# First batch of the second attention: its second half of scores in two projection banks, both weighings read ahead of the sums, POOL's four differences in a row

## Chip, cores, metric

The kernel runs on 1 core of one Trainium2 chip. The metric is the device time of one execution, in microseconds (us), as the median of several runs.

## What is computed

Thirty-two batches of 128 tokens with 128 features pass through two layers, each a cross attention and a mixture of experts. The change lies in the second layer's attention (16 heads of 64):

```python
x = x + _L0_xattn_ref(_layernorm(x), ctx_768, mask_BxS_bk0, L0_xattn_Wq, L0_xattn_Wkv)
x = x + _L0_ffn_ref(_layernorm(x), ...)          # 8 experts, top 2
x = x + _L1_xattn_ref(_layernorm(x), ctx_768, w_q, w_k, w_v, w_out, b_out)
x = x + _L1_ffn_ref(_layernorm(x), ...)          # 16 experts, top 1, and a shared one

def _L1_xattn_ref(x, cond, w_q, w_k, w_v, w_out, b_out):
    q = (x @ w_q).reshape(B, SQ, 16, 64)
    k = (cond @ w_k).reshape(B, SKV, 16, 64)
    v = (cond @ w_v).reshape(B, SKV, 16, 64)
    attn = softmax(einsum('bqhd,bkhd->bhqk', q, k) / 8)
    return einsum('bhqk,bkhd->bqhd', attn, v).reshape(B, SQ, 1024) @ w_out + b_out
```

## The kernel before, in words

The whole program is written out by hand, one instruction list for each engine, held together by semaphores. Five stages follow one another: the first attention, the first experts, the second attention (batches 0 to 31, steps of `attention()` on each engine), and the second experts with the shared one. Batch b of the second attention has two halves of eight heads (h = 0, 1), and each half two groups of four heads (g = 0 to 3). For a half:

- `coarse_half(b, h)` (TensorE, line 1311): scores in bf16 into the banks mf[0:2]. `half_max` (VectorE, L2164) takes their maxima over the keys; there is one pair of such banks, so a coarse half waits until the half before it has been reduced.
- `turn(b)` (TensorE, L1347 and L1353): transposes the maxima of batch b+1 and the normalized rows of a later batch into mf; ScalarE copies them out (L1762, L1772, L1773, L1776). At b = 0 the rows are those of batches 2 and 3, at b = 1 those of batch 4, so `turn(1)` waits for `normal_before(4)`.
- `score_half(b, h)` (L1284, then L1294 with the negated maxima): scores in fp32 into the banks S1 = sf[0:2]; ScalarE's `exponential` (L1755) writes them to pT[h] and counts `exp_done`. With one S1, a score half waits for the exponential of the half before it.
- `high_half` (VectorE L2158 or, for h = 0 of batches 1 to 6, ScalarE L1815): pT[h] rounded to bf16 in ph[h].
- `low_halves(b, h)` (POOL, L870, two instructions): pl[h] = pT[h] - ph[h].
- `weigh(b, g)` (TensorE, L1330, 16 matmuls): the weights, high and low, times the values, into the single bank of; `evacuate(b, g)` (VectorE, L2148 and L2149) divides by the row sums and frees the bank. So `weigh` of a group waits for `evacuate` of the group before it (`pv_free`) and for one of POOL's differences (`pl_done`).

Queries (`q0`, `q1`, L1223), transposed outputs (`oT0`, `oT1`, L1218) and the output product (`y`, L1214) go through three projection banks, J1 = sf[2], sf[3], jf; sf[2] and sf[3] are the two that the title names.

Beside this run the sums of the first experts: POOL's `fetch(t)` (L859, two gathers) brings two expert rows for batch t, VectorE's `combine(t)` (L2194, two instructions, all operands in SBUF) adds them to x, `stats_before` and `aggregate_before` (L2205, L2209, L2210) take mean and variance, POOL's `root_before(t)` (L878) the inverse root, VectorE's `normal_before(t)` (L2217) the normalized rows, and POOL's `bias(t)` (L890) adds the output bias to x once `normal_before(t)` has read it. `normal_after` (L2233) does the same for the rows after the attention.

Orders written out by hand around the change:

- TensorE: ... coarse(0,1), q1 of batch 1, products of scores (0,0), turn(-1), shift of (0,0), coarse(1,0), scores (0,1), coarse(1,1), turn(0), weigh(0,0), q0 of batch 2, weigh(0,1); then step b = 1: scores (1,0), coarse(2,0), weigh(0,2), q1 of batch 2, oT0 of batch 0, weigh(0,3), scores (1,1), coarse(2,1), weigh(1,0), oT1 of batch 0, q0 of batch 3, weigh(1,1), y of batch 0, turn(1); then step 2 with scores (2,0), coarse(3,0), weigh(1,2), q1 of batch 3, oT0 of batch 1, weigh(1,3), and so on.
- POOL in step 1: root_before(4), low_halves(1,0), bias(4), fetch(7), low_halves(1,1); in step 2: root_before(5), root_after(0), low_halves(2,0), bias(5), fetch(8), low_halves(2,1).
- VectorE in step 1: evacuate(0,2), half_max(2,0), evacuate(0,3), statistics of batch 5, evacuate(1,0), half_max(2,1), high_half(1,1), evacuate(1,1), combine(6), the output and statistics of batch 0, normal_before(5).

Of the kernel before, what the change touches and what calls it, by code (L numbers as in the profile page):

```python
# [10 lines left out]
ACT = mybir.ActivationFunctionType  # L11
# [3 lines left out]
P = 128  # L15
# [129 lines left out]
def inside(b):  # L145
    return 0 <= b < NB
# [132 lines left out]
def build(nc, a, out):  # L279
    ctx = ExitStack()  # L280
    with ctx:
# [157 lines left out]
        bank = [sf[:, n, :] for n in range(4)] + [mf[:, n, :] for n in range(2)] + [of[:, :]]  # L439
        cf0, cf = sf[:, 0, 0:P // 2].bitcast(BF16), mf[:, 0, 0:P // 2].bitcast(BF16)  # L440
        S1, M1p, J1 = sf[:, 0:2, :], mf, [sf[:, 2, :], sf[:, 3, :], jf[:, :]]
        s_bank, st_bank, pj_bank = bank[0:2], bank[2:4], bank[4:6]
        o_bank = [of[:, 0:QH * (D1 + 1)], mf[:, 0, 0:QH * (D1 + 1)]]
        g_bank, y_bank = bank[0:4], (of[:, 0:DM], jf[:, 0:DM])
# [86 lines left out]
        with nc.Block(no_gpsimd_drain=True) as block:  # L531
# [200 lines left out]
            def _(pool):  # L732
# [140 lines left out]
                def attention():  # L873

                    def root_before(t):

                        pool.wait_ge(L1.veA_done, t + 1)
                        nc.gpsimd.tensor_tensor(rsA[:, t:t + 1], veA[:, t:t + 1], mhalf[:, 0:1], ALU.pow)\  # L878
                            .then_inc(L1.rsA_done, 1)

                    def root_after(n):

                        pool.wait_ge(L1.veF_done, n + 1)
                        nc.gpsimd.tensor_tensor(rstd[:, n:n + 1], veF[:, n:n + 1], mhalf[:, 0:1], ALU.pow)\
                            .then_inc(L1.rsF_done, 1)

                    def bias(t):

                        pool.wait_ge(L1.xn_ready, t + 1)
                        nc.gpsimd.tensor_tensor(x[:, t, :], x[:, t, :], bo1[:, :], ALU.add).then_inc(L1.biased, 1)  # L890

                    def score(q):

                        c = slice(QH * q, QH * q + QH)
                        pool.wait_ge(sel_ready, NROUNDS + q + 1)
                        nc.gpsimd.tensor_tensor(v2[:, c], einv[:, :], v1[:, c], ALU.pow).then_inc(scored, 1)

                    pool.wait_ge(tiles_ready, 3)
                    pool.wait_ge(cleared, 16 * NCLEAR)
                    store_tiles(0, SOON_TILES[0] + X0)  # L900
                    fetch(0)
                    store_tiles(SOON_TILES[0] + X0, SOON_TILES[0] + X0 + 4)
                    fetch(1)
                    store_tiles(SOON_TILES[0] + X0 + 4, SOON_TILES[0] + X0 + 8)
                    root_before(0)
                    store_tiles(SOON_TILES[0] + X0 + 8, SOON_TILES[2] + 4)
                    root_before(1)
                    store_tiles(SOON_TILES[2] + 4, SOON_TILES[2] + X0)
                    fetch(2)
                    store_tiles(SOON_TILES[2] + X0, SOON_TILES[2] + X0 + 4)  # L910
                    fetch(3)
                    store_tiles(SOON_TILES[2] + X0 + 4, SOON_TILES[2] + X0 + 12)
                    bias(0)
                    bias(1)
                    store_tiles(SOON_TILES[2] + X0 + 12, NT0 - X0)
                    root_before(2)
                    root_before(3)
                    store_tiles(NT0 - X0, NT0)
                    fetch(4)
                    fetch(5)  # L920
                    low_halves(0, 0)
                    fetch(6)
                    bias(2)
                    low_halves(0, 1)
                    bias(3)
                    for b in range(1, NB):
                        if inside(b + 3):
                            root_before(b + 3)
                        if inside(b - 2):
                            root_after(b - 2)  # L930
                        if b % QH == 0 and 0 <= b // QH - 2:
                            score(b // QH - 2)
                        if inside(b):
                            low_halves(b, 0)
                        if inside(b + 3):
                            bias(b + 3)
                        if inside(b + 6):
                            fetch(b + 6)
                        if inside(b):
                            low_halves(b, 1)  # L940
                    score(NQD - 2)
                    root_after(LAST - 1)
                    root_after(LAST)
                    score(NQD - 1)
# [23 lines left out]
            def _(pe):  # L968
# [231 lines left out]
                def fill(name, n):  # L1200

                    what, h, p = name[:-1], int(name[-1] == "1"), n % 2
                    bk, use = FILL1[name, n]
                    ps = J1[bk]
                    need(pe, L1.pj_free[bk], use)
                    if name == "q0" and n >= 3:
                        pe.wait_ge(L1.k_free, 2 * (n - 1) + 2)
                    if name == "oT0" and inside(n + 2):
                        pe.wait_ge(L1.k_free, 2 * (n + 2) + 2)
                    if name == "y":  # L1210
                        L1.free(pe, "oT0", n)
                        L1.free(pe, "oT1", n)
                        for c in range(NCH):
                            last = nc.tensor.matmul(ps[:, 0:DM], oT[:, c, :], wo1[:, c, :], start=(c == 0), stop=(c == NCH - 1))  # L1214
                    elif what == "oT":
                        pe.wait_ge(L1.pv_free, 4 * n + 2 * h + 2)
                        for c in range(4):
                            last = nc.tensor.transpose(ps[:, c * P:(c + 1) * P],  # L1218
                                                       o1[p][:, 8 * h + 2 * c:8 * h + 2 * c + 2, :], ident[:, :])
                    else:  # L1220
                        pe.wait_ge(L1.moved_done, MOVED1[XMOVE[n]] + 1)
                        for c in range(4):
                            last = nc.tensor.matmul(ps[:, c * P:(c + 1) * P], wq1[:, (4 * h + c) * P:(4 * h + c + 1) * P],  # L1223
                                                    xrn[p][:, :], start=True, stop=True)
                    last.then_inc(L1.pj_full[bk], 1)
# [47 lines left out]
                def score_products(b, h):  # L1273

                    p = b % 2
                    L1.free(pe, f"q{h}", b)
                    keys_there(b, h, L1.kf_io[p])
                    if h == 0 and b >= NKV:
                        pe.wait_ge(L1.v_free, 2 * b + 2)
                    need(pe, L1.exp_done, 2 * b + h)  # L1280
                    for n in range(4):
                        for r in range(2):
                            rr = slice(D1 * r, D1 * r + D1)
                            nc.tensor.matmul(S1[:, r, n * P:(n + 1) * P], kT[p][rr, 4 * h + n, :], qT[p][rr, 4 * h + n, :],  # L1284
                                             start=(n == 0), stop=False)

                def score_shift(b, h):
# [3 lines left out]
                    for n in range(4):  # L1291
                        for r in range(2):
                            rr = slice(D1 * r, D1 * r + D1)
                            last = nc.tensor.matmul(S1[:, r, n * P:(n + 1) * P], sel1[rr, 4 * h + n, :], cT1[p][rr, :],  # L1294
                                                    start=False, stop=(n == 3))
                            if n == 3:
                                last.then_inc(L1.s_full, 1)
# [305 lines left out]
            def _(act):  # L1603
# [146 lines left out]
                def exponential(b, h):  # L1750

                    act.wait_ge(L1.s_full, 4 * b + 2 * h + 2)
                    if b >= 1:
                        act.wait_ge(L1.pl_done, 4 * (b - 1) + 2 * h + 2)
                    nc.scalar.activation(pT[h][:, :, :, :].rearrange("p r c n -> p r (c n)"), S1, ACT.Exp, scale=D1 ** -0.5)\  # L1755
                        .then_inc(L1.exp_done, 1)

                def turn(b):
# [152 lines left out]
            def _(dve):  # L1911
# [353 lines left out]
                def attention():  # L2265
# [6 lines left out]
                    high_half(0, 0)  # L2272
                    half_max(1, 1)
                    high_half(0, 1)
                    combine(4)
                    stats_before(4)
                    aggregate_before(4)
                    evacuate(0, 0)
                    combine(5)
                    evacuate(0, 1)  # L2280
                    normal_before(4)

                    for b in range(1, LIGHT):
                        evacuate(b - 1, 2)
                        half_max(b + 1, 0)
                        evacuate(b - 1, 3)
                        stats_before(b + 4)
                        aggregate_before(b + 4)
# [1 line left out]
                        half_max(b + 1, 1)  # L2290
                        high_half(b, 1)
                        evacuate(b, 1)
                        if inside(b - 2):
                            normal_after(b - 2)
                        combine(b + 5)
# [339 lines left out]
```

## Time and profile before

| | |
|---|---|
| median of 3 runs | 936.29 us (935.24, 936.29, 941.63) |
| profiled execution | 932.35 us, span of its trace 930.7 us |
| TensorE | busy 844.5 us, 91% of the span, granted clock 0.964 on average |
| VectorE, ScalarE, POOL | 601.0, 547.6 and 476.1 us busy |
| second attention | first exponential at 353.7 us, last at 766.3 us |

All times below are microseconds from the start of the span. The durations of a row are those of one instruction, or of the stretch that a group of neighbours takes; a bracket tells how long the engine stood idle before it, and who ended that.

### The profile page before, as it was taken

What the parts mean: (1) busy time and instruction counts of PE and PEld (TensorE: products, weight loads), DVE (VectorE), ACT (ScalarE), POOL (GpSimd) and SP (SyncE); (2) the same over time, 40 slices, a digit from 0 to 9 for tenths busy, and PEclk for the clock granted to TensorE, in tenths of its full rate; (3) what the DMA queues carried; (4) which work ended last, traced back from release to release, by engine and by line L of the source; (5) the groups of instructions that cost most, each with busy time, mean ns of one, the idle gap of its engine ahead of it and who ended that gap; (6) DMA issues with size and microseconds to landing.
All of it is one profiled execution on the core that took longest, in us unless ns stands there. A gap on an engine that the chain in (4) does not pass through costs nothing.

```text
span 930.7 us, 31432 instructions
## 1 busy us (share of the span) xinstructions
PE 844.5 (91%) x11898; PEld 715.5 (77%) x11898; DVE 601.0 (65%) x1729; ACT 547.6 (59%) x1209; POOL 476.1 (51%) x580
## 2 busy tenths in 40 slices
PE   7899988877899997998999999999999998888886
PEld 3565555545579996888989999999999988868775
DVE  5887767634565656876777777777777677424443
ACT  3887776533377784665666666656656653226553
POOL 7123334353624437665665565575564444644555
PEclk8999999867799998999999999999999999999999
DMA  5444554501744433441545210110010001344330
GB/s 151 118 116 144 164 172 148 155 32 65 263 147 130 127 108 101 143 130 37 184 146 172 77 30 17 31 31 20 28 31 19 12 2 32 124 143 118 103 95 24
DMA packets 85860, 90.51 MB, mean 97 GB/s; under 512 B 15233, under 2 KB 70728, under 8 KB 84946
## 3 DMA queue, kind: packets, MB, share of 16 engines
q1 hardware_dynamic: 76658, 71.26, 24.9%
q0 software_dynamic: 8256, 17.01, 5.8%
q8 instruction: 99, 1.62, 0.7%
q14 instruction: 47, 0.39, 0.1%
q10 hardware_dynamic: 800, 0.24, 0.1%
HBM read 44.70 MB, written 42.01 MB: 93 GB/s over the span
## 4 chain that ended last, share of the span: by engine, by line
PE 75%; DVE 10%; issue 6%; another core or an unknown queue 3%; ACT 2%; DMA 1%; POOL 1%; SPq 0%; ACTq 0%; DVEq 0%; POOLq 0%
PE of L1330 8%; PE sf L1284 7%; PE jf L1214 5%; PE sf L1588 5%; PE sf L1255 4%; PE sf L1519 4%; PE mf L1241 4%; PE sf L1510 3%; PE jf L1223 3%; PE sf L1421 3%; PE sf L1223 3%; PE sf L1015 3%; DVE cmx L1934 2%; PE mf L1311 2%
## 5 line engine op out<-in xcount | busy, mean ns | idle before, releaser
L870 POOL TENSOR_TENSOR pl<-pT,ph 128x512 bf16<-128x512 f32 x128 | 146.0, 1165 | 111.4 <-DVE ph L2158 103.0
L796 POOL DMA_INDIRECT buf<-gu,slots x64 | 63.1, 986 | 90.5 <-PE of L1061 65.2
L2164 DVE TENSOR_REDUCE cmxb<-mf 128x8 bf16<-128x1024 f32 x64 | 78.2, 1222 | 45.5 <-PE mf L1311 40.8
L1934 DVE TENSOR_REDUCE cmx<-mf 128x8 bf16<-128x1024 f32 x64 | 78.3, 1224 | 42.5 <-PE mf L1042 27.8
L1755 ACT ACTIVATE pT<-sf 128x1024 f32<-128x1024 f32 x64 | 66.6, 1041 | 30.6 <-PE sf L1294 30.6
L1652 ACT ACTIVATE pTf<-sf 128x1024 f32<-128x1024 f32 x64 | 62.5, 1021 | 28.2 <-remote 14.7
L1284 PE MATMUL sf<-qTs,kTs 64*128 64x128 f32 x1024 | 75.2, 287 | 1.6 <-issue 1.6
L859 POOL DMA_INDIRECT gb<-eo,slots x64 | 65.7, 1027 | 18.4 <-issue 14.8
L959 POOL DMA_INDIRECT out<-rows x47 | 46.3, 985 | 49.7 <-DVE rows L2567 39.5
L1284 PEld LDWEIGHTS sf<-qTs,kTs 64*128 64x128 f32 x1024 | 62.8, 189 | 7.1 <-issue 2.0
L1214 PE MATMUL jf<-wo,oT 128*128 128x128 f32 x496 | 62.9, 280 | 0.0
L1214 PEld LDWEIGHTS jf<-wo,oT 128*128 128x128 f32 x496 | 57.8, 192 | 0.0
L2149 DVE TENSOR_TENSOR o1s<-of,rden 128x256 f32<-128x256 f32 x125 | 53.1, 425 | 4.3
L1855 ACT ACTIVATE hT<-sf,qTs 128x128 f32<-128x128 f32 x142 | 44.6, 367 | 14.5 <-PE sf L1510 12.5
L2559 DVE TENSOR_TENSOR hT<-kTs,sf 128x256 f32<-128x256 f32 x47 | 19.8, 421 | 47.1 <-ACT kTs L1905 29.3
L1588 PE MATMUL sf<-xsT,qTs 128*128 128x128 f32 x376 | 49.7, 275 | 0.0
L1061 PE MATMUL of<-pTf,vq 128*32 128x128 f32 x1024 | 41.1, 293 | 7.3 <-ACT oh L1658 4.5
L849 POOL DMA_DIRECT2D eo<-rows x35 | 19.6, 559 | 53.3 <-DVE rows L2492 52.8
L1588 PEld LDWEIGHTS sf<-xsT,qTs 128*128 128x128 f32 x376 | 45.6, 191 | 0.0
L1726 ACT CAST kTb<-mf 128x512 bf16<-128x512 f32 x24 | 14.1, 586 | 53.5 <-PE sf L1241 53.5
L1519 PE MATMUL sf<-dn,hT 128*128 x284 | 44.1, 278 | 1.6 <-DVE rows L2492 1.1
L1510 PE MATMUL sf<-qTs 128*128 128x128 f32 x284 | 44.4, 279 | 0.9 <-ACT hT L1855 0.8
(334 smaller groups left out, 2711.6 us busy)
## 6 DMA issues: line engine op xcount, KB each, us to landing
buf<-zero SPq DMA_DIRECT2D x12, 516.0 KB, 6.4
rows<-buf SPq DMA_DIRECT2D x47, 129.0 KB
buf<-zero SPq DMA_DIRECT2D x22, 256.0 KB, 3.7
eo<-zero SPq DMA_DIRECT2D x22, 256.0 KB
ctxT<-in_ctxP SPq DMA_DIRECT2D x24, 192.0 KB
rows<-buf SPq DMA_DIRECT2D x71, 64.0 KB
gu<-in_gu SPq DMA_DIRECT2D x4, 1024.0 KB
kept<-kTs SPq DMA_DIRECT2D x6, 512.0 KB
```

The lines of the kernel that those rows point to most:

```text
L796: nc.gpsimd.indirect_dma_start(out=buf0[:, :], out_offset=bass.IndirectOffsetOnAxis(ap=slots0[:, k, b:b + 1], axis=0), in_=xna0[:, b, :], ...
L859: nc.gpsimd.indirect_dma_start(out=gb[t % 4 * 2 + k][:, :], out_offset=None, in_=eo0[0:ZROW + P, :], in_offset=bass.IndirectOffsetOnAxis(a ...
L870: nc.gpsimd.tensor_tensor(pl[h][:, :, c, :], pT[h][:, :, c, :], ph[h][:, :, c, :], ALU.subtract)\
L1214: last = nc.tensor.matmul(ps[:, 0:DM], oT[:, c, :], wo1[:, c, :], start=(c == 0), stop=(c == NCH - 1))
L1284: nc.tensor.matmul(S1[:, r, n * P:(n + 1) * P], kT[p][rr, 4 * h + n, :], qT[p][rr, 4 * h + n, :], start=(n == 0), stop=False)
L1330: last = nc.tensor.matmul(ps[:, j * (D1 + 1):(j + 1) * (D1 + 1)], pp[h][:, r, n, :], va1[p][part][:, QH * g + j, :], start=(m == 0), stop= ...
L1510: last = nc.tensor.matmul(s_bank[n % 2][:, f * P:(f + 1) * P], stage0[n % DEEP][:, f * P:(f + 1) * P], xsT0[n % DEEP], start=True, stop=True)
L1519: last = nc.tensor.matmul(st_bank[n % 2][:, 0:DM], hT1[n % DEEP][:, f, :], w2r[:, bass.ds(e, 1), f, :].squeeze(1), start=(f == 0), stop=(f ...
L1588: last = nc.tensor.matmul(g_bank[n % DEEP][:, c * P:(c + 1) * P], stage[n % DEEP][:, c * P:(c + 1) * P], xsT1[n % DEEP], start=True, stop= ...
L1755: nc.scalar.activation(pT[h][:, :, :, :].rearrange("p r c n -> p r (c n)"), S1, ACT.Exp, scale=D1 ** -0.5)\
L1934: nc.vector.reduce_max(to, mf[:, :, :].rearrange("p c (j k) -> p c j k", j=QH), AX.X)\
L2164: nc.vector.reduce_max(cmx1[b % 2][:, :].rearrange("p (r k) -> p r k", r=2)[:, :, 4 * h:4 * h + 4], M1p[:, :, :].rearrange("p r (c k) -> p ...
```

## The change

`scores_of(b, h)` names the banks of a score half: S1 for all but (0,1), which gets sf[2:4], two of the three projection banks. The products of (0,1) therefore don't wait for the exponential of (0,0); in exchange q0 of batch 2, the next user of sf[2], waits until both exponentials of batch 0 have been read (`exp_done` 2). On VectorE evacuate(0,0) and evacuate(0,1) come before combine(4); combine(5) goes behind half_max(2,0) of step 1, and normal_before(4) behind evacuate(1,1) of step 1. On POOL the four differences of batch 0 stand in a row, fetch(6) behind them, and bias(2) and bias(3) go behind low_halves(1,0), ahead of bias(4) and fetch(7).

```diff
--- before.py
+++ after.py
@@ -439,6 +439,11 @@
         bank = [sf[:, n, :] for n in range(4)] + [mf[:, n, :] for n in range(2)] + [of[:, :]]
         cf0, cf = sf[:, 0, 0:P // 2].bitcast(BF16), mf[:, 0, 0:P // 2].bitcast(BF16)
         S1, M1p, J1 = sf[:, 0:2, :], mf, [sf[:, 2, :], sf[:, 3, :], jf[:, :]]
+
+        def scores_of(b, h):
+
+            return sf[:, 2:4, :] if (b, h) == (0, 1) else S1
+
         s_bank, st_bank, pj_bank = bank[0:2], bank[2:4], bank[4:6]
         o_bank = [of[:, 0:QH * (D1 + 1)], mf[:, 0, 0:QH * (D1 + 1)]]
         g_bank, y_bank = bank[0:4], (of[:, 0:DM], jf[:, 0:DM])
@@ -919,10 +924,8 @@
                     fetch(4)
                     fetch(5)
                     low_halves(0, 0)
+                    low_halves(0, 1)
                     fetch(6)
-                    bias(2)
-                    low_halves(0, 1)
-                    bias(3)
                     for b in range(1, NB):
                         if inside(b + 3):
                             root_before(b + 3)
@@ -932,6 +935,9 @@
                             score(b // QH - 2)
                         if inside(b):
                             low_halves(b, 0)
+                        if b == 1:
+                            bias(2)
+                            bias(3)
                         if inside(b + 3):
                             bias(b + 3)
                         if inside(b + 6):
@@ -1203,6 +1209,8 @@
                     bk, use = FILL1[name, n]
                     ps = J1[bk]
                     need(pe, L1.pj_free[bk], use)
+                    if name == "q0" and n == 2:
+                        pe.wait_ge(L1.exp_done, 2)
                     if name == "q0" and n >= 3:
                         pe.wait_ge(L1.k_free, 2 * (n - 1) + 2)
                     if name == "oT0" and inside(n + 2):
@@ -1277,11 +1285,12 @@
                     keys_there(b, h, L1.kf_io[p])
                     if h == 0 and b >= NKV:
                         pe.wait_ge(L1.v_free, 2 * b + 2)
-                    need(pe, L1.exp_done, 2 * b + h)
+                    if b >= 1:
+                        pe.wait_ge(L1.exp_done, 2 * b + h)
                     for n in range(4):
                         for r in range(2):
                             rr = slice(D1 * r, D1 * r + D1)
-                            nc.tensor.matmul(S1[:, r, n * P:(n + 1) * P], kT[p][rr, 4 * h + n, :], qT[p][rr, 4 * h + n, :],
+                            nc.tensor.matmul(scores_of(b, h)[:, r, n * P:(n + 1) * P], kT[p][rr, 4 * h + n, :], qT[p][rr, 4 * h + n, :],
                                              start=(n == 0), stop=False)
 
                 def score_shift(b, h):
@@ -1291,7 +1300,7 @@
                     for n in range(4):
                         for r in range(2):
                             rr = slice(D1 * r, D1 * r + D1)
-                            last = nc.tensor.matmul(S1[:, r, n * P:(n + 1) * P], sel1[rr, 4 * h + n, :], cT1[p][rr, :],
+                            last = nc.tensor.matmul(scores_of(b, h)[:, r, n * P:(n + 1) * P], sel1[rr, 4 * h + n, :], cT1[p][rr, :],
                                                     start=False, stop=(n == 3))
                             if n == 3:
                                 last.then_inc(L1.s_full, 1)
@@ -1752,7 +1761,7 @@
                     act.wait_ge(L1.s_full, 4 * b + 2 * h + 2)
                     if b >= 1:
                         act.wait_ge(L1.pl_done, 4 * (b - 1) + 2 * h + 2)
-                    nc.scalar.activation(pT[h][:, :, :, :].rearrange("p r c n -> p r (c n)"), S1, ACT.Exp, scale=D1 ** -0.5)\
+                    nc.scalar.activation(pT[h][:, :, :, :].rearrange("p r c n -> p r (c n)"), scores_of(b, h), ACT.Exp, scale=D1 ** -0.5)\
                         .then_inc(L1.exp_done, 1)
 
                 def turn(b):
@@ -2272,17 +2281,17 @@
                     high_half(0, 0)
                     half_max(1, 1)
                     high_half(0, 1)
+                    evacuate(0, 0)
+                    evacuate(0, 1)
                     combine(4)
                     stats_before(4)
                     aggregate_before(4)
-                    evacuate(0, 0)
-                    combine(5)
-                    evacuate(0, 1)
-                    normal_before(4)
 
                     for b in range(1, LIGHT):
                         evacuate(b - 1, 2)
                         half_max(b + 1, 0)
+                        if b == 1:
+                            combine(5)
                         evacuate(b - 1, 3)
                         stats_before(b + 4)
                         aggregate_before(b + 4)
@@ -2290,6 +2299,8 @@
                         half_max(b + 1, 1)
                         high_half(b, 1)
                         evacuate(b, 1)
+                        if b == 1:
+                            normal_before(4)
                         if inside(b - 2):
                             normal_after(b - 2)
                         combine(b + 5)
```

## Rows read from the trace of the kernel before

**Rows 1.** Page: busy time, share of the span, instructions, for TensorE

```profile
PE 844.5 (91%) x11898; PEld 715.5 (77%) x11898; DVE 601.0 (65%) x1729; ACT 547.6 (59%) x1209; POOL 476.1 (51%) x580
```

**Rows 2.** Busy time by stretch: stretch, length, engines, granted clock, DMA share, GB/s

```profile
350.00:355.00 5.00, 2.44 (x39) 1.95 (x40) 0.60 (x1) 1.55 (x3) 3.22 (x4) 1.00 0.38 106
355.00:360.00 5.00, 3.68 (x43) 3.36 (x44) 4.08 (x5) 2.18 (x6) 2.76 (x3) 0.50 0.25 68
```

**Rows 3.** Timeline of TensorE, 352 to 374: start, us, instruction, [idle before]

```profile
352.84 0.40 PE L1311 MATMUL mf<-kTb,qTb 64*128 64x128 bf16 x8
354.89 1.97 PE L1284 MATMUL sf<-qTs,kTs 64*128 64x128 f32 x16 [1.65 <-issue]
...
359.03 0.29 PE L1347 MATMUL mf<-identb,cmxb 128*128 128x128 bf16 x1 [1.32 <-DVE cmxb L2164]
...
362.69 1.16 PE L1284 MATMUL sf<-qTs,kTs 64*128 64x128 f32 x16
...
366.01 0.19 PE L1330 MATMUL of<-va10h,ph 128*128 128x65 bf16 x1 [1.71 <-DVE o1s L2149]
...
372.97 0.19 PE L1330 MATMUL of<-va11h,ph 128*128 128x65 bf16 x1 [0.63 <-DVE o1s L2149]
```

**Rows 4.** Timeline of ScalarE, 353 to 358

```profile
353.72 1.02 ACT L1755 ACTIVATE pT<-sf 128x1024 f32<-128x1024 f32 x1 [1.27 <-PE sf L1294]
...
355.10 0.60 ACT L1716 COPY qTs<-jf 128x512 f32<-128x512 f32 x1
357.32 1.02 ACT L1755 ACTIVATE pT<-sf 128x1024 f32<-128x1024 f32 x1 [1.61 <-PE sf L1294]
```

**Rows 5.** Timeline of VectorE, 355 to 379

```profile
355.17 1.22 DVE L2164 TENSOR_REDUCE cmxb<-mf 128x8 bf16<-128x1024 f32 x1 [4.58 <-remote]
...
357.74 1.22 DVE L2164 TENSOR_REDUCE cmxb<-mf 128x8 bf16<-128x1024 f32 x1 [0.75 <-PE mf L1311]
358.89 1.01 DVE L2158 CAST ph<-pT 128x1024 bf16<-128x1024 f32 x1
359.82 0.79 DVE L2194 SCALAR_TENSOR_TENSOR rows<-gb,wt,rows 128x128 f32<-128x128 f32 x2
...
361.81 3.50 DVE L2194 SCALAR_TENSOR_TENSOR rows<-gb,wt,rows 128x128 f32<-128x128 f32 x2
365.44 0.42 DVE L2149 TENSOR_TENSOR o1s<-of,rden 128x256 f32<-128x256 f32 x1
365.78 0.34 DVE L2217 TENSOR_SCALAR xn<-rows,mvA,rsA 128x128 f32<-128x128 f32 x1
...
375.02 2.09 DVE L2194 SCALAR_TENSOR_TENSOR rows<-gb,wt,rows 128x128 f32<-128x128 f32 x2
...
377.97 0.35 DVE L2217 TENSOR_SCALAR xn<-rows,mvA,rsA 128x128 f32<-128x128 f32 x1
```

**Rows 6.** Timeline of POOL, 357 to 377

```profile
357.08 2.26 POOL L870 TENSOR_TENSOR pl<-pT,ph 128x512 bf16<-128x512 f32 x2 [2.95 <-DVE ph L2158]
...
362.01 0.47 POOL L890 TENSOR_TENSOR rows<-rows,bo 128x128 f32<-128x128 f32 x1
362.42 2.27 POOL L870 TENSOR_TENSOR pl<-pT,ph 128x512 bf16<-128x512 f32 x2
...
369.17 1.00 POOL L859 DMA_INDIRECT gb<-eo,slots  x1 [0.16 <-issue]
370.48 0.96 POOL L859 DMA_INDIRECT gb<-eo,slots  x1 [0.31 <-issue]
374.64 2.32 POOL L870 TENSOR_TENSOR pl<-pT,ph 128x512 bf16<-128x512 f32 x2 [3.21 <-DVE ph L2158]
376.92 0.61 POOL L878 TENSOR_TENSOR rsA<-veA,mhalf 128x1 f32<-128x1 f32 x1
```

**Rows 7.** Chain of waits in order of time: start, us, what

```profile
377.19 0.59 PE of L1330 x16
...
379.19 0.48 PE of L1330 x16
```

## The prediction, made before the changed kernel was run

> **What bounds the kernel now.** I read the page first: TensorE is busy 91% of the span [rows 1], so a stretch gives something back only if TensorE stands idle in it. Next the granted clock by stretches: at the start of the second attention, 350 to 355, TensorE is busy 2.44 of 5 us, and in the next 5 us the granted clock is 0.50, the 1.2 GHz level, after full speed before [rows 2]. Then TensorE's timeline there [rows 3]. Four waits are to be seen: 1.65 us before scores (0,1) at 354.89, 1.32 before turn(0) at 359.03, 1.71 before weigh(0,2) at 366.01, and 0.63 before weigh(1,1) at 372.97. The first is listed as "issue", but the exponential of (0,0) ends at 353.72 + 1.02 = 354.74 [rows 4], 0.15 before TensorE starts: that is the wait for S1 that the change removes. The second waits for half_max(1,1), 357.74 + 1.22 [rows 5]. The third waits for evacuate(0,1), which ends at 365.44 + 0.42 = 365.86 because combine(5) stood in front of it for 3.50 us [rows 5]. From 366.01 to weigh(1,2) at 377.19 [rows 7] TensorE rests only those 0.63 us, and from there the light steps repeat. So the start is a ladder of single waits, and I place the changed order on the same ladder, with these durations, up to weigh(1,2) and weigh(1,3) of step 2: what they gain or lose, everything behind them gains or loses.
>
> **Scores (0,1) in sf[2:4].** They follow coarse(1,0) at 353.24 and take 1.16 + 0.4 at full clock [rows 3], so end near 354.8, not 357.3. ScalarE has the copies of q1 until 355.10 + 0.60, so the exponential of (0,1) runs 355.7 to 356.7, not 357.32 to 358.34 [rows 4]. But coarse(1,1) waits for half_max(1,0), which starts at 355.17 though coarse(1,0) is recorded as ended at 353.24 [rows 3, 5]: its release comes 1.9 us late and has nothing to do with S1. I leave it there: 355.17 + 1.22 gives coarse(1,1) at 356.5, and half_max(1,1), behind high_half(0,0), starts at 357.03 in place of 357.74. **Turn(0), weigh(0,0) and q0 of batch 2 come 0.7 earlier**: all that is left of 1.65. The added wait of q0 of batch 2 for both exponentials has behind it, on TensorE, everything from weigh(0,1) on; it ends at 356.7 and q0 would start at 360.5 - 0.7 = 359.8, so it costs nothing. If the release of (0,1) is late by 1.9 as well, the exponential ends at 357.7, still in time. Without that cover it would cost what it lacks. high_half(0,1) arrives at 358.15, between the two differences of (0,0), which end at 359.34 [rows 6]; where it met the second before, it took 1.01, to 359.90 [rows 5]. Bounds 358.85 and 359.90; I take the later, the row's own. It hurts nobody: POOL's differences of (0,1) then run 359.9 to 362.2 in place of 362.42 to 364.69 [rows 6], both ahead of weigh(0,2) and weigh(0,3).
>
> **Weighings ahead of the sums.** weigh(0,1) ends near 362.2 (before, 362.7), evacuate(0,1) at 362.85, not 365.86. combine(4), 0.79 [rows 5], and the statistics of batch 4, 0.7, follow to 364.25. scores (1,0) start 0.6 earlier, coarse(2,0) ends at 363.6, and weigh(0,2) starts there, not at 366.01: **a lead of 2.4 us**, the largest that the change makes. evacuate(0,2) ends at 364.9, half_max(2,0) at 366.0.
>
> **combine(5) at its new place** reaches VectorE at 365.95. POOL then works: fetch(6), behind the four differences, ends at 362.35 + 2.4 = 364.75, root_before(4) at 365.5, and low_halves(1,0), whose ph is ready at 365.4, takes 365.5 to 367.8; bias(2) and bias(3), 0.47 each [rows 6], follow to 368.7. Combines and POOL's arithmetic obstruct each other: alone two combines take 0.79; beside the differences at 374.64 they took 2.09; beside bias and both differences, 362.01 to 364.69, they took 3.50, the first until POOL's third instruction had ended [rows 5, 6]. I take 2.09, since the neighbour is again a pair of differences: combine(5) ends at 368.0. evacuate(0,3) stands behind it and ends at 368.65, and weigh(1,0), for which TensorE would be ready at 367.7, waits for it. **1.0 of the lead is gone.**
>
> **A rule of the Trainium skill** bears on this: SBUF — State Buffer, section "Who interferes with whom", says that VectorE with two SBUF inputs and GpSimd reading SBUF exclude each other, and that whoever issues first has the port for its whole instruction. By that rule combine(5) would wait only for the difference already under way, near the 2.09 that I took. The trace agrees on the blocking but not on its length: the combine of 361.81 began before the bias of 362.01 and yet let three POOL instructions pass [rows 5, 6].
>
> **The rest of step 1.** weigh(1,0) 368.75 to 369.25, oT1 and q0 of batch 3 to 370.75, weigh(1,1) to 371.35, y (1.87) to 373.2. VectorE meanwhile: evacuate(1,0) to 370.1, half_max(2,1) to 371.3, high_half(1,1) to 371.9, evacuate(1,1) to 372.5, normal_before(4), 0.34 [rows 5], to about 372.65 with the overlap of neighbours. The 0.63 wait before weigh(1,1) is gone, turn(1) isn't held, and scores (2,0) could start 2.2 us earlier than before.
>
> **What is late next** is an edit that looks free. bias(4) waits for normal_before(4). Before, that ended at 366.1, ahead of bias(4) at 368.56; now it ends at 372.65, at the end of step 1, and POOL stands at bias(4) with fetch(7) and low_halves(1,1) queued behind. From 372.65: 0.03, bias 0.46, 0.15, fetch(7) 2.27 (369.17 to 371.44), 0.03, first difference 1.16, 0.15 to TensorE [rows 6]: 4.25 us, so weigh(1,2) starts at **376.9 against 377.19** [rows 7], with TensorE idle for some 2 us before it. low_halves(1,1) then ends at 378.0, not 376.96; root_before(5), 0.61 [rows 6], at 378.6; normal_before(5) at 378.9 (377.97 + 0.35 before [rows 5]); and evacuate(1,2), behind it on VectorE, at 379.5. weigh(1,3) waits for that: **379.6 against 379.19** [rows 7], 0.4 later. Nothing behind has a time of its own, so 0.4 stays.
>
> bias(2) and bias(3) behind low_halves(1,0) cost nothing: their reader is the sum of the output of batch 2, two steps on, and POOL stands waiting anyway. What they can cost is their share in holding combine(5).
>
> **Sum.** -1.65 at scores (0,1), of which 0.7 reaches turn(0); lead 2.4 at weigh(0,2); 1.0 lost to combine(5); 0.7 regained at weigh(1,1); about 2.5 lost to bias(4) and root_before(5): net +0.4. Against the profiled execution 932.35 + 0.4 = 932.75; against the median of the runs 936.29 + 0.4 = 936.7.
>
> **Rivals.**
> (a) Part of the lead is kept: combine(5) is not held (0.79, not 2.09), everything to normal_before(4) is 1.3 earlier, and the chain through bias(4) with it: weigh(1,3) at 378.3, 0.9 us less: 935.4. For it: the combines beside a gather took 0.79. Against: low_halves(1,0) lies right on its new place. If the late release of 1.9 us vanishes too, 1 us more: 934.4.
> (b) Slower: combine(5) is held through both differences and both added biases, to 368.7 + 0.15, and ends at 369.6, 1.6 later; weigh(1,3) follows: +2.0, 938.3. For it: 3.50 us in row 361.81. It decides as soon as combine(5) ends later than 367.6, where weigh(1,3) is even with before.
> (c) The clock falls once more, since TensorE idles 1.0 and 2.0 us in step 1. The half-speed stretch of before made scores (0,1) 1.97 instead of 1.16 [rows 3], and the weighing, queries and transposes beside it longer in proportion, 2.4 together: +2.8, 939.1. Against it: the waits of 1.7 at 364 left the clock up.
> (d) The change does nothing of what it says, since scores (0,1) are held by something else at "issue"; then only the new orders act, with evacuate(0,1) early and bias(4) late: +0.5 to +1, 937.
>
> **Chances.** Forecast 0.42, (a) 0.28, (b) 0.17, (c) 0.06, (d) 0.07. All of them lie within 4 us, 0.4%; 1%, 9.4 us, is about what a measurement of this kernel can tell from no change, so 0.96 for no change and 0.02 for either side. The range, 933.3 to 939.3, reaches from (a) with its late release gone to (c), and takes in that two of the three runs before differ by 1 us and the third by 5.
>
> **What would show it.** Scores (0,1) directly behind coarse(1,0); the wait before weigh(0,2) gone; combine(5) near 2 us beside L870; a wait of some 1 us before weigh(1,0); POOL idle for 3 to 4 us before bias(4), fetch(7) after 372.7, and TensorE idle about 2 us before weigh(1,2). The prediction is wrong if weigh(1,2) starts well before 376, which needs normal_before(4) to end before 371.8, or if a step behind it takes up the difference.

## The result and the profile after

The changed kernel takes 940.92 us (median of 20 runs, 932.98 to 949.39), the kernel before 935.26 (20 runs, 930.25 to 945.68). The ratio is 1.005, 95% interval 1.0027 to 1.0073: slower by 4.7 us, 2.5 to 6.8, where 0.4 was forecast. The ratio comes from the fast runs alone, without those of a slower state that some executions fall into whatever the kernel, so it is less than that of the two medians. The forecast time was 936.7 us, in a range from 933.3 to 939.3. Single runs of either spread over 15 us, so I compare places inside traces, counted from the last addition of the first experts, whose code is the same in both: 346.40 before, 353.82 in the profiled execution after. The 7.42 us between them arose before anything that was changed, and I subtract it below. From there to the exponential of (4,0) the profiled executions took 53.7 us before and 56.2 after: 2.5 us lost. The rest of the difference of their spans, 930.7 and 944.4, lies in stretches with the same instructions in the same order: 7.4 us before that stretch and 3.8 behind it. That the change causes any of those isn't shown.

After, timeline of TensorE (start, us, instruction, idle before); what answers is [rows 3] and [rows 7]:

```profile
361.18 1.13 PE L1293 MATMUL sf<-qTs,kTs 64*128 64x128 f32 x16
...
363.96 0.40 PE L1320 MATMUL mf<-kTb,qTb 64*128 64x128 bf16 x8 [1.25 <-DVE cmxb L2173]
365.68 0.23 PE L1356 MATMUL mf<-identb,cmxb 128*128 128x128 bf16 x1 [1.32 <-DVE cmxb L2173]
...
366.80 1.13 PE L1231 MATMUL sf<-xrn,wq 128*128 128x128 f32 x8
...
369.88 0.20 PE L1339 MATMUL of<-va10h,ph 128*128 128x65 bf16 x1
...
373.33 0.19 PE L1339 MATMUL of<-va10h,ph 128*128 128x65 bf16 x1 [1.38 <-DVE o1s L2158]
...
375.99 0.19 PE L1339 MATMUL of<-va11h,ph 128*128 128x65 bf16 x1 [0.47 <-DVE o1s L2158]
...
384.65 0.23 PE L1339 MATMUL of<-va11h,ph 128*128 128x65 bf16 x1 [2.60 <-POOL pl L875]
385.52 2.06 PE L1231 MATMUL jf<-xrn,wq 128*128 128x128 f32 x8
...
389.76 0.19 PE L1339 MATMUL of<-va11h,ph 128*128 128x65 bf16 x1 [1.45 <-DVE o1s L2158]
```

Scores (0,1), at 361.18, follow coarse(1,0) with no wait; the 1.65 us are gone. A wait of 1.25 now stands before coarse(1,1), for half_max(1,0), and turn(0) at 365.68 - 7.42 = 358.26 is 0.8 earlier than before. The 1.71 before weigh(0,2), at 369.88, are gone too. In their place stand 1.38 before weigh(0,3), 0.47 before weigh(1,0), 2.60 before weigh(1,2) and 1.45 before weigh(1,3). Now POOL after, against [rows 6]:

```profile
364.50 4.97 POOL L875 TENSOR_TENSOR pl<-pT,ph 128x512 bf16<-128x512 f32 x4 [2.93 <-DVE ph L2167]
...
379.93 0.49 POOL L895 TENSOR_TENSOR rows<-rows,bo 128x128 f32<-128x128 f32 x1 [4.37 <-DVE xn L2226]
381.14 1.00 POOL L864 DMA_INDIRECT gb<-eo,slots  x1 [0.72 <-DVE rows L2203]
382.45 0.96 POOL L864 DMA_INDIRECT gb<-eo,slots  x1 [0.31 <-issue]
383.43 2.27 POOL L875 TENSOR_TENSOR pl<-pT,ph 128x512 bf16<-128x512 f32 x2
385.65 0.58 POOL L883 TENSOR_TENSOR rsA<-veA,mhalf 128x1 f32<-128x1 f32 x1
386.20 0.55 POOL L889 TENSOR_TENSOR rstd<-veF,mhalf 128x1 f32<-128x1 f32 x1
386.72 2.26 POOL L875 TENSOR_TENSOR pl<-pT,ph 128x512 bf16<-128x512 f32 x2
```

The four differences stand in a row. Then POOL is idle for 4.37 us before the bias of 379.93: that is bias(4), released by normal_before(4) (xn). Behind it come fetch(7), low_halves(1,1), root_before(5), root_after(0) and low_halves(2,0), with hardly a gap. VectorE after, against [rows 5]:

```profile
374.23 1.06 DVE L2203 SCALAR_TENSOR_TENSOR rows<-gb,wt,rows 128x128 f32<-128x128 f32 x2
...
379.51 0.34 DVE L2226 TENSOR_SCALAR xn<-rows,mvA,rsA 128x128 f32<-128x128 f32 x1
...
386.27 2.79 DVE L2226 TENSOR_SCALAR xn<-rows,mvA,rsA 128x128 f32<-128x128 f32 x1 [4.77 <-POOL rsA L883]
388.98 0.17 DVE L2157 RECIPROCAL rden<-of 128x4 f32<-128x4 f32 x1
```

379.51 is normal_before(4). 386.27 is normal_before(5): it waits 4.77 us for root_before(5), and then takes 2.79 us, where the other takes 0.34. It ends at 389.06, when low_halves(2,0) has just ended at 388.98, and evacuate(1,2), for which weigh(1,3) waits, starts only then. Stretches after, against [rows 2]:

```profile
360.00:365.00 5.00, 2.40 (x48) 1.93 (x48) 2.41 (x3) 3.19 (x5) 1.77 (x3) 1.00 0.10 27
365.00:370.00 5.00, 4.19 (x79) 3.92 (x80) 3.24 (x8) 1.98 (x6) 4.85 (x5) 1.00 0.49 161
...
380.00:385.00 5.00, 2.40 (x45) 2.09 (x44) 1.29 (x6) 2.50 (x4) 3.96 (x5) 0.96 0.14 40
385.00:390.00 5.00, 3.55 (x34) 3.30 (x32) 3.70 (x4) 1.56 (x3) 4.68 (x7) 0.70 0.00 0
```

The first two cover the stretch that had a granted clock of 0.50 before (355 to 360 in [rows 2], here 362.4 to 367.4): that half-speed stretch is gone, and q0 of batch 2, at 366.80, takes 1.13 us where it took 1.80. From 380 to 385 TensorE is busy 2.40 of 5 us, and in the next 5 the granted clock is 0.70 on average: a part at the 1.2 GHz level. The eight matmuls of q1 at 385.52 take 2.06 us, for 1.13 at full clock.

### The profile page after: what moved, and what is told of

Same layout as the page of the kernel before. It is cut to its first block, busy times and chain, and to the rows that moved or that the text cites. A ratio compares the mean times of both kernels' runs of the same rounds, so it can differ in the third digit from the quotient of the medians.

```text
span 944.4 us, 31432 instructions
## 1 busy us (share of the span) xinstructions
PE 848.3 (90%) x11898; PEld 717.4 (76%) x11898; DVE 600.1 (64%) x1729; ACT 547.2 (58%) x1209; POOL 475.7 (50%) x580
## 4 chain that ended last, share of the span: by engine, by line
PE 73%; DVE 10%; issue 7%; another core or an unknown queue 3%; ACT 3%; DMA 1%; POOL 1%; SPq 0%; DVEq 0%; ACTq 0%; POOLq 0%
PE of L1339 8%; PE sf L1293 7%; PE jf L1222 5%; PE sf L1597 5%; PE sf L1263 4%; PE mf L1249 4%; PE sf L1528 4%; PE sf L1519 3%; PE jf L1231 3%; PE sf L1430 3%; PE sf L1231 3%; PE sf L1021 2%; DVE cmx L1943 2%; PE mf L1320 2%
## 5 line engine op out<-in xcount | busy, mean ns | idle before, releaser
L1661 ACT ACTIVATE pTf<-sf 128x1024 f32<-128x1024 f32 x64 | 62.5, 1021 | 28.4 <-remote 14.2
```

## The experiments

All ran on another chip than the prediction's profile, which does the same work faster: the kernel before has a median of 856.69 there in the first set and 857.6 in the second. So both kernels were run there too. Expected stretches that were worked out from the first chip's traces (e1 to e4) have to be read with that in mind. The stretch in the table goes from the last addition of the first experts to the exponential of (4,0), from one trace each; the waits are TensorE's, in us, before the weighing named.

| run | median us | ratio to before, 95% | stretch | (0,2) | (1,0) | (1,2) | (1,3) |
|---|---|---|---|---|---|---|---|
| c_before | 859.51 (one run) | | 48.0 | 1.78 | 0 | 0 | 0 |
| c_after | 862.97 | 1.0057 (1.0037 to 1.0078) | 55.0 | 0 | 1.16 | 2.59 | 3.03 |
| e5: before, norm4 late | 864.27 | 1.0068 (1.0039 to 1.0098) | 55.1 | 1.78 | 0 | 2.59 | 2.35 |
| e4: after, root5 early | 860.19 | 1.0046 (1.0011 to 1.0081) | 51.7 | 0 | 2.53 | 2.61 | 0 |
| e1: after, norm4 early | 856.46 | 0.9984 (0.9954 to 1.0014) | 48.5 | 0 | 1.17 | 0 | 0.06 |
| e2: after, bias4 last | 856.48 | 0.9988 (0.9958 to 1.0017) | 48.0 | 0 | 1.17 | 0 | 0 |
| e3: before, scores only | 857.68 | 1.0015 (0.9989 to 1.0041) | 48.0 | 1.77 | 0 | 0 | 0 |
| e6: after, all mended | 856.73 | 0.9987 (0.9959 to 1.0014) | 47.2 | 0 | 0 | 0 | 0.06 |

### c_before and c_after: both kernels on this chip

> The kernel before, unchanged, for a trace on the chip of the experiments (whose times lie near 857 us, not 936). Stretch from the last addition of the first experts to the exponential of (4,0): e1, e2, e3 gave 48.5, 48.0, 48.0 here. If the mended orders gain what the ladder says, 49.0 to 50.3; if they gain nothing, 47.8 to 48.5.

> The changed kernel, unchanged, on the same chip. e4 gave 51.7 with the wait before weigh(1,3) taken away. Theory A (bias(4), then normal_before(5) behind root_before(5) and held by low_halves(2,0)): weigh(1,2) waits about 2.6, weigh(1,3) 1.4 or more, stretch 52.5 to 54.5; time 3 to 5 us above the kernel before. Rival (the order of e4 changed nothing, its 51.7 is that of the changed kernel): 51.5 to 52.0.

c_before's 48.0 says that the mended orders of e1 to e3 gain nothing in this stretch. c_after's 55.0 lies just above the range of theory A and clear of the rival's 51.5 to 52.0; its time is 4.9 us above the kernel before, inside the 3 to 5 expected; its wait before weigh(1,3) is 3.03 us, twice that on the first chip. In c_before the only one of the table's four waits is that before weigh(0,2) (weigh(0,1) has 0.76 us, also behind an evacuation):

```profile
326.74 0.19 PE L1330 MATMUL of<-va10h,ph 128*128 128x65 bf16 x1 [1.78 <-DVE o1s L2149]
```

### e1: normal_before(4) early

```diff
                         stats_before(b + 4)
                         aggregate_before(b + 4)
+                        if b == 1:
+                            normal_before(4)
                         evacuate(b, 0)
...
                         evacuate(b, 1)
-                        if b == 1:
-                            normal_before(4)
```

> The changed kernel with one edit: normal_before(4) stands behind the statistics of batch 5 in step 1, ahead of evacuate(1,0), not behind evacuate(1,1). Measure: from the last addition of the first experts (L2492 before, L2503 after) to the exponential of (4,0): 53.7 us before the change, 56.2 after it. Theory A (the loss comes from bias(4), which waits for normal_before(4) with fetch(7), low_halves(1,1) and root_before(5) behind it on POOL): the stretch falls to 51.3 to 52.5, POOL's 4.37 us before the third bias are gone, and so are the 2.60 us before weigh(1,2) and the 1.45 before weigh(1,3); total 3 to 5 us below the changed kernel. Rival B (the loss comes from combine(5) at its new place or from the two banks): the stretch stays above 55.

POOL, then TensorE's weigh(1,2) and weigh(1,3):

```profile
328.15 0.46 POOL L895 TENSOR_TENSOR rows<-rows,bo 128x128 f32<-128x128 f32 x1 [0.83 <-DVE xn L2226]
```

```profile
333.33 0.20 PE L1339 MATMUL of<-va11h,ph 128*128 128x65 bf16 x1
...
336.14 0.19 PE L1339 MATMUL of<-va11h,ph 128*128 128x65 bf16 x1
```

The waits before weigh(1,2) and weigh(1,3) are gone, and POOL's wait before bias(4) has shrunk to 0.83 us. The stretch is 48.5, far from the rival's 55. It lies below the 51.3 to 52.5 expected, which were numbers of the slower chip; against c_after it is 6.5 us less, and the ratio falls from 1.0057 to 0.9984, a little more than the 3 to 5 us expected. A new wait of 0.49 us stands before q1 of batch 3, behind a combine(6) that takes 3.38 us. Moving one small instruction takes the loss away.

### e2: bias(4) last on POOL

```diff
-                        if inside(b + 3):
+                        if b > 1 and inside(b + 3):
                             bias(b + 3)
...
                             low_halves(b, 1)
+                        if b == 1:
+                            bias(4)
```

> The changed kernel with one edit: bias(4) stands behind low_halves(1,1) on POOL; normal_before(4) stays late on VectorE. Theory A (what costs is what is queued behind bias(4)): as e1, stretch 51.3 to 52.5. Rival C (normal_before(4) late is itself the cost, through turn(1) or VectorE's order): stretch 55 or more. Part of a loss may stay, since VectorE's normal_before(4) can meet low_halves(1,1) on the way, up to 1.1 us.

VectorE, then POOL, then TensorE's weigh(1,2):

```profile
333.05 0.86 DVE L2228 TENSOR_SCALAR xn<-rows,mvA,rsA 128x128 f32<-128x128 f32 x1
```

```profile
334.90 0.51 POOL L895 TENSOR_TENSOR rows<-rows,bo 128x128 f32<-128x128 f32 x1
```

```profile
335.83 0.20 PE L1341 MATMUL of<-va11h,ph 128*128 128x65 bf16 x1
```

VectorE's order is that of the change, and normal_before(4) is as late (24.5 us after the last addition, 24.4 in c_after), and yet the stretch is 48.0 and the ratio 0.9988. So it is not the lateness itself that costs, but what was queued on POOL behind the instruction that waits for it.

### e3: the scores' banks alone

```diff
-nc.tensor.matmul(S1[:, r, n * P:(n + 1) * P], kT[p]...
+nc.tensor.matmul(scores_of(b, h)[:, r, n * P:(n + 1) * P], kT[p]...
...
+                    if name == "q0" and n == 2:
+                        pe.wait_ge(L1.exp_done, 2)
```

> The kernel before with the first part of the change alone: scores (0,1) in sf[2:4], q0 of batch 2 behind both exponentials; VectorE's and POOL's orders as before. Theory A: turn(0) 0.7 us earlier, and combine(5) reaches VectorE ahead of bias(2), so that it takes 0.8 and not 3.5; weigh(0,2) then waits only for POOL, 2.2 us earlier than before: stretch 51.4 to 52.3 against 53.7 before. Rival D: combine(5) is held all the same, then only 0 to 0.7 is gained: 53.0 to 53.7. Rival E (the banks cost something of their own): over 53.9.

Rival D, at its lower end: 48.0, as c_before. VectorE in c_before, then in e3:

```profile
319.62 1.01 DVE L2158 CAST ph<-pT 128x1024 bf16<-128x1024 f32 x1
320.55 0.79 DVE L2194 SCALAR_TENSOR_TENSOR rows<-gb,wt,rows 128x128 f32<-128x128 f32 x2
...
322.55 3.50 DVE L2194 SCALAR_TENSOR_TENSOR rows<-gb,wt,rows 128x128 f32<-128x128 f32 x2
```

```profile
314.00 1.35 DVE L2166 CAST ph<-pT 128x1024 bf16<-128x1024 f32 x1
315.27 0.79 DVE L2202 SCALAR_TENSOR_TENSOR rows<-gb,wt,rows 128x128 f32<-128x128 f32 x2
...
317.27 3.50 DVE L2202 SCALAR_TENSOR_TENSOR rows<-gb,wt,rows 128x128 f32<-128x128 f32 x2
```

The last addition is at 309.49 in c_before and 304.19 in e3, so high_half(0,1) starts 0.32 earlier in e3 (9.81 for 10.13), but in both it ends 0.55 us behind low_halves(0,0), whose place hasn't changed: it takes 0.34 more in e3, and combine(4) follows at 11.08 there and at 11.06 in c_before. POOL's order is untouched and combine(5) is held for 3.50 us as before. The expectation had left that cast out.

### e4: root_before(5) early

```diff
-                        if inside(b + 3):
+                        if b != 2 and inside(b + 3):
                             root_before(b + 3)
...
+                        if b == 1:
+                            root_before(5)
                         if inside(b + 6):
                             fetch(b + 6)
```

> The changed kernel with one edit: root_before(5) stands behind bias(4) and ahead of fetch(7) on POOL, not behind low_halves(1,1). It leaves the 2.60 us before weigh(1,2) (theory: fetch(7) and low_halves(1,1) behind bias(4)) and takes away normal_before(5) late and held by low_halves(2,0), 2.79 us for 0.35. Theory A: wait before weigh(1,2) 2.6 to 3.3, wait before weigh(1,3) under 0.3, normal_before(5) 0.35 us, stretch 53.2 to 54.3. Rival F (the 2.60 are all of the loss, the wait before weigh(1,3) comes from something else): 55.5 or more.

VectorE and TensorE in c_after, then in e4:

```profile
336.61 2.79 DVE L2226 TENSOR_SCALAR xn<-rows,mvA,rsA 128x128 f32<-128x128 f32 x1 [4.76 <-POOL rsA L883]
```

```profile
334.99 0.20 PE L1339 MATMUL of<-va11h,ph 128*128 128x65 bf16 x1 [2.59 <-POOL pl L875]
...
340.09 0.19 PE L1339 MATMUL of<-va11h,ph 128*128 128x65 bf16 x1 [3.03 <-DVE o1s L2158]
340.96 2.08 PE L1293 MATMUL sf<-qTs,kTs 64*128 64x128 f32 x16
```

```profile
324.59 3.54 DVE L2205 SCALAR_TENSOR_TENSOR rows<-gb,wt,rows 128x128 f32<-128x128 f32 x2
...
334.26 0.35 DVE L2228 TENSOR_SCALAR xn<-rows,mvA,rsA 128x128 f32<-128x128 f32 x1
```

```profile
337.49 0.20 PE L1341 MATMUL of<-va11h,ph 128*128 128x65 bf16 x1 [2.61 <-POOL pl L875]
338.20 2.06 PE L1233 MATMUL jf<-xrn,wq 128*128 128x128 f32 x8
...
340.90 0.26 PE L1341 MATMUL of<-va11h,ph 128*128 128x65 bf16 x1
```

With its root there in time normal_before(5) takes 0.35 us for 2.79, the wait before weigh(1,3) is gone, and the one before weigh(1,2) is the same. The stretch, 51.7, is 3.2 us below c_after's; it lies below the 53.2 to 54.3 expected, which were numbers of the first chip. This divides c_after's 6.9 us: weigh(1,2) starts 2.3 later than in c_before, weigh(1,3) 5.5, weigh(2,0) 7.0; the three steps are bias(4) with its queue (2.3), normal_before(5) (3.2), and the lower clock on scores (2,1), 2.08 us for 1.16, and on the shift and coarse half beside them (1.6). In e4 the first remains, and a spell at the lower clock on q1 and the transposes (weigh(1,2) to weigh(1,3) take 3.4 us, 1.9 in c_before): 3.7 in all. The split is read from places in single traces; in time e4 (1.0046) and c_after (1.0057) can't be told apart, so only the traces show what normal_before(5) costs.

One thing more differs. In c_after the clock also falls at q0 of batch 2 (2.05 us for 1.13), as it does in e1, e2, e3 and e6, all with the scores' new banks; in c_before and e5, with the old ones, and in e4 it doesn't. weigh(0,2) comes 15.6 us after the last addition in c_after and 14.2 in e4, but combine(5) is then held for 3.54 us in e4 and 2.17 in c_after, and normal_before(4) starts at 24.3 and 24.4: what the clock spared was lost to combine(5).

### e5: the kernel before, with normal_before(4) late

```diff
                     evacuate(0, 1)
-                    normal_before(4)
...
                         evacuate(b, 1)
+                        if b == 1:
+                            normal_before(4)
```

> The kernel before with one part of the change alone: normal_before(4) behind evacuate(1,1) of step 1; scores, weighings and POOL's order as before. Theory A: POOL stands before bias(4) until normal_before(4), weigh(1,2) waits 2 us or more, normal_before(5) is late: stretch 2.5 to 5 us above that of the kernel before, time 0.3 to 0.6% above. Rival (the loss needs the other edits beside it): stretch within 1 us of the kernel before.

POOL, then VectorE, then TensorE:

```profile
333.29 0.49 POOL L890 TENSOR_TENSOR rows<-rows,bo 128x128 f32<-128x128 f32 x1 [5.44 <-DVE xn L2217]
334.50 1.00 POOL L859 DMA_INDIRECT gb<-eo,slots  x1 [0.72 <-DVE rows L2194]
```

```profile
339.62 2.79 DVE L2217 TENSOR_SCALAR xn<-rows,mvA,rsA 128x128 f32<-128x128 f32 x1 [4.75 <-POOL rsA L878]
```

```profile
338.01 0.20 PE L1330 MATMUL of<-va11h,ph 128*128 128x65 bf16 x1 [2.59 <-POOL pl L870]
...
343.11 0.22 PE L1330 MATMUL of<-va11h,ph 128*128 128x65 bf16 x1 [2.35 <-DVE o1s L2149]
```

This one move gives the whole loss: 7.1 us in the stretch (well above the 2.5 to 5 expected, which had no lower clock in it, while scores (2,1) take 2.08 us here too), 1.0068 in time (0.3 to 0.6% were expected), and the same three signs as the change. The other edits don't cause it, and hardly soften it.

### e6: all mended

```diff
                     aggregate_before(4)
+                    combine(5)
...
                         half_max(b + 1, 0)
-                        if b == 1:
-                            combine(5)
```

and the edits of e1 and e2.

> The changed kernel with normal_before(4) behind the statistics of batch 5, bias(4) behind low_halves(1,1), and combine(5) directly behind the statistics of batch 4, beside fetch(6) and ahead of low_halves(1,0). Theory A: no wait of 1.2 before weigh(1,0) (combine(5) 0.8, not 2.1), none before weigh(1,2) and weigh(1,3): stretch 46.3 to 47.4, against 48.0 of e2; time 1 to 3 us below the kernel before, at the edge of what five rounds tell. Rival (combine(5) then delays evacuate(0,2), or something else is next): 47.8 to 48.5.

```profile
325.98 0.81 DVE L2205 SCALAR_TENSOR_TENSOR rows<-gb,wt,rows 128x128 f32<-128x128 f32 x2
```

combine(5) beside fetch(6) takes 0.81 us, not 2.17 as in c_after, and the wait before weigh(1,0) is gone. The stretch is 47.2, 0.8 below c_before. The time, 0.9987 with an interval from 0.9959 to 1.0014, doesn't tell that from nothing: no version here was shown to beat the kernel before.

## Why the prediction was wrong

**Right.** Places in the time of before: turn(0) was forecast at 358.3 and came at 358.26; normal_before(4) to end at 372.65, ended at 372.43; POOL idle 3 to 4 us before bias(4), was a little more, 4.37; TensorE idle about 2 us before weigh(1,2), was 2.60; weigh(1,2) at 376.9, came at 377.23 (377.19 in [rows 7], its first matmul at 377.12); root_before(5) to end at 378.6, ended at 378.81. That bias(4) gives the lead back was the main finding, and e1, e2 and e5 show it.

**Right by luck.** weigh(1,0) was put at 368.75 and came at 375.99 - 7.42 = 368.57, but by misses that cancel. weigh(0,2) came at 369.88 - 7.42 = 362.46, not at 363.6, since the ladder kept the half-speed durations of [rows 2] that the change itself took away. That lead went again because evacuate(0,2) started only at 372.54, 2 us after weigh(0,2) was recorded as done. And combine(5), which was to take up 1.0 of the lead with 2.09 us, took 1.06. On the other chip combine(5) is as forecast: 2.17 us, and a wait of 1.16 before weigh(1,0). So rival (b) found no place, and the condition of rival (a), combine(5) not held, was met on the first chip without its gain.

**Small miss.** The chain behind normal_before(4) was put at 4.25 us and took 4.8: fetch(7) began 0.72 us behind the bias, not 0.15.

**The step that failed** is "root_before(5), 0.61 [rows 6], at 378.6; normal_before(5) at 378.9", with weigh(1,3) at 379.6 against 379.19 as what follows from it. The place was right, the size was not: this is the term of the sum "about 2.5 lost to bias(4) and root_before(5)". normal_before(5) was given its 0.35 us and took 2.79, because POOL, behind root_before(5), had root_after(0) and low_halves(2,0) ready. The same text prices combine(5) by just such an obstruction, and then lets an instruction of VectorE pass for free at the one moment when POOL has a backlog. weigh(1,3) came at 389.76 - 7.42 = 382.34. In the timeline of before its first matmul is at 379.02 (the 379.19 of [rows 7] is where its neighbour ended), so it is 3.3 us late, not 0.4, and scores (2,1) behind it are as late. The chain of waits after the change runs through that instruction (start, us, what):

```profile
385.65 0.59 POOL rsA L883
386.24 0.03 issue
386.27 2.79 DVE xn L2226
389.06 0.10 DVE rden L2157
```

e4 shows the link: root_before(5) earlier, no obstruction, no wait.

**Rival (c), at 0.06, came true in part beside it.** The clock fell after the idle stretch before weigh(1,2); c_after, e4 and e5 have the fall as well, at slightly different places; c_before, e1, e2, e3 and e6, without that idle stretch, have none there. It cost about 1.6 us in c_after. In the first chip's profile the fall lay on q1 and the transposes, and TensorE still waited 1.45 us behind them for evacuate(1,2), so there it cost nothing: it is no part of those 3.3 us. The prediction priced it as an alternative to the forecast; all four traces with such a wait before weigh(1,2) show the fall behind it, so it belonged beside the forecast.

**"Nothing behind has a time of its own"** didn't quite hold: turn(2) had a wait of 1.09 us for normal_after before and has none after, which gives back 0.8 us net; 2.5 of 3.3 stay. The median says 4.7, with 2.5 as the lower end of its interval. On the other chip trace and time say 6.9 and 4.9 (3.2 to 6.7). How much of 4.7 is more than those 2.5 isn't settled by one trace of each.

**Why the loss depends on the chip.** From the start of normal_before(4) to weigh(1,2) it takes 5.14 and 5.13 us in the two traces of the changed kernel (25.69 to 30.83 after the last addition, and 24.40 to 29.53). But the kernel before reaches weigh(1,2) at 30.72 on the first chip and at 27.27 on the other, where the releases that come 1 to 2 us late on the first are not seen. Up to weigh(1,2) that chain thus costs 0.1 us on the one and 2.3 on the other.

## What to carry to other kernels

When an instruction is moved later, look up who waits for it on another in-order engine and price everything queued behind that waiter, to the end of the queue's backlog, not only the first reader. A backlog is also work that will run without a gap: any VectorE instruction with all its operands in SBUF that lands in it should be priced at anything up to the length of the backlog (2.79 us for 0.35 here). And where a forecast has a wait of TensorE like the 2.6 us here, the lower clock behind it belongs in the sum and not among the rivals: it came in all four traces with that wait, and cost nothing in the first chip's and 1.6 us in c_after.

## What the runs showed of the hardware

How long VectorE is held beside POOL isn't given by its first neighbour. A combine that started 0.29 us after the first of two differences (c_after, 323.47 and 323.18) got in between them, its two instructions 2.17 in all; one that started 0.12 us after (e4, 324.59 and 324.47) was held through both and the two biases behind them, 3.54; in c_before and e3, started ahead of a bias, it took 3.50 both times. normal_before(5) started at 386.27, beside the root of 386.20, and let both differences behind it pass as well. The Trainium skill, SBUF — State Buffer, section "Who interferes with whom", has the two engines exclude each other on the ports that they share for a whole instruction, whoever issues first going first. The traces agree that they exclude each other; that the waiting one isn't served when that instruction ends, but after up to three more, is what these rows add.

The two chips differ by 8% on the same program (935 and 857 us). A light step, exponential (4,0) to (5,0), takes 11.6 us on the first and 10.5 on the other. On the first, some releases by TensorE arrive up to 2.0 us after the recorded end of the matmul: half_max(1,0) starts at 355.17 behind a coarse half ended at 353.24 [rows 3, 5]. It starts at the same place after the change, 362.59 - 7.42, though the coarse half is recorded as ended 0.7 later, so the recorded end isn't what it hangs on. In the light steps of before the one behind weigh(b,1) is late by 1.24 to 1.29 us each time, and turn(b+1) waits 1.09 us for normal_after; the second chip shows neither, and its step is 1.1 us shorter. What delays them was not found.
